# Expert results stored by SyncE in sorted order and gathered by GpSimd, in place of a scatter by GpSimd and a reload

## The reference, cut to what matters

```python
shared_enc = _expert_stack(x, sW1, sb1, sW2, sb2).sum(0)          # 128 -> 512 -> 128, gelu
weights = jax.nn.softmax(x @ gW + gb, axis=-1)                    # 15 experts
topv, topi = jax.lax.top_k(weights, TOP_K)                        # TOP_K = 3
gated = (jax.nn.one_hot(topi, E_ROUTER) * topv[..., None]).sum(axis=-2)
router_out = _expert_stack(x, rW1, rb1, rW2, rb2)                 # 128 -> 256 -> 128 each
router_enc = jnp.einsum('ebtd,bte->btd', router_out, gated)
return shared_enc + router_enc + x                                # then the last layer norm
```

## Time and profile before

| what | us |
|---|---|
| median of 3 timed runs | 285.67 (283.55 to 286.89) |
| the profiled execution, its span (what lies around it is not shown) | 319.6 |
| busy: PE / DVE / ACT / POOL | 241.1 / 221.6 / 192.2 / 179.0 |

### The profile page before, as it was taken

One profiled execution on the slowest core, in us unless ns is written; L12 is line 12 of the kernel. 1 busy time (PEld: TensorE's weight loads), 2 busy tenths in 40 slices (PEclk: granted clock), 3 DMA queues, 4 the chain that ended last, 5 costly groups with the idle time before them and its releaser, 6 DMA issues.

```text
span 319.6 us, 7117 instructions
## 1 busy us (share of the span) xinstructions
PE 241.1 (75%) x2283; PEld 179.8 (56%) x2283; DVE 221.6 (69%) x630; ACT 192.2 (60%) x423; POOL 179.0 (56%) x166
## 2 busy tenths in 40 slices
PE   6989989877988767996761299688868867785970
PEld 3676868655535434452451156586857757674960
DVE  6777999989999998998520497043444434856875
ACT  4697997549976976754470350344554546563665
POOL 6132755330666738985677467135656566665752
PEclk9999999999997998998978589799999999999778
DMA  7672830124000002952211133123132263354462
GB/s 218 217 213 46 181 128 2 37 67 133 2 0 2 0 4 62 378 215 49 86 58 50 44 101 108 41 61 101 53 99 76 75 187 90 91 168 123 150 185 90
DMA packets 38597, 31.89 MB, mean 100 GB/s; under 512 B 12864, under 2 KB 31552, under 8 KB 38432
## 3 DMA queue, kind: packets, MB, share of 16 engines
q1 hardware_dynamic: 34608, 23.90, 26.6%
q0 software_dynamic: 3520, 7.27, 6.7%
q10 hardware_dynamic: 432, 0.27, 0.3%
HBM read 19.95 MB, written 11.47 MB: 98 GB/s over the span
## 4 chain that ended last, share of the span: by engine, by line
PE 44%; DVE 27%; issue 14%; ACT 4%; another core or an unknown queue 4%; POOL 4%; DMA 1%; DVEq 0%; SPq 0%; ACTq 0%
PE psum L994 12%; PE psum L985 9%; PE psum L783 5%; DVE prob_sums L1496 4%; PE psum L763 4%; DVE maxes L1490 3%; PE psum L977 2%; PE psum L568 2%; DVE prob_sums L1410 2%; POOL x_srt L1986 2%; PE psum L585 1%; DMA xT<-x_t 1%; DVE turned_room L1421 1%; DVE maxes L1405 1%
## 5 line engine op out<-in xcount | busy, mean ns | idle before, releaser
L2047 POOL DMA_INDIRECT y_tok<-k_heads,y_rows x62 | 62.7, 1012 | 50.8 <-ACT k_heads L1327 34.4
L1319 ACT ACTIVATE k_heads<-psum,k_heads 128x128 f32<-128x128 f32 x124 | 38.7, 365 | 38.5 <-PE psum L985 33.6
L1986 POOL DMA_INDIRECT x_srt<-v_blocks,slot x48 | 48.0, 1000 | 21.3 <-issue 17.2
L994 PE MATMUL psum<-k_heads 128*128 128x128 f32 x248 | 42.4, 295 | 18.0 <-issue 12.1
L1823 DVE COPY k_heads<-psum 128x128 f32<-128x128 f32 x62 | 17.8, 289 | 48.9 <-PE psum L977 32.7
L994 PEld LDWEIGHTS psum<-k_heads 128*128 128x128 f32 x248 | 34.2, 200 | 21.9 <-issue 15.2
L985 PE MATMUL psum<-k_heads 128*128 128x128 f32 x248 | 40.6, 288 | 5.2 <-DVE k_heads L1823 4.2
L1963 POOL TENSOR_TENSOR k_heads<-k_heads,inv_sums 128x1024 f32<-128x1024 f32 x14 | 27.1, 1939 | 24.0 <-DVE inv_sums L1503 23.9
L985 PEld LDWEIGHTS psum<-k_heads 128*128 128x128 f32 x248 | 33.8, 198 | 8.5 <-DVE k_heads L1823 7.4
L1951 POOL TENSOR_TENSOR probs<-probs,inv_sums 128x512 f32<-128x512 f32 x16 | 16.8, 1050 | 28.9 <-DVE inv_sums L1415 28.7
L1327 ACT ACTIVATE k_heads<-psum,k_heads 128x128 f32<-128x128 f32 x62 | 22.9, 370 | 11.3 <-PE psum L994 9.1
(11 more groups left out here) (191 smaller groups left out, 530.1 us busy)
## 6 DMA issues: line engine op xcount, KB each, us to landing
expert_w<-e_w SPq DMA_DIRECT2D x1, 4369.0 KB
k_heads<-x_srt SPq DMA_DIRECT2D x62, 65.0 KB
q_heads<-y_tok SPq DMA_DIRECT2D x8, 256.0 KB
x_srt<-pad SPq DMA_DIRECT2D x16, 65.0 KB
xT<-x_t SPq DMA_DIRECT2D x4, 256.0 KB, 5.1
ctxT_k<-ctx_k SPq DMA_DIRECT2D x2, 512.0 KB, 5.5
v_scr<-v_rows SPq DMA_DIRECT2D x4, 256.0 KB, 2.8
ctxT_v<-ctx_v SPq DMA_DIRECT2D x2, 512.0 KB, 5.0
```

Source lines behind the costliest of these rows:

```text
L994: mm = pe.matmul(bank[6 + t % 2][:, 0:E], h_tile[:, t % 2, a, :], tile_weights(t)[:, FE + E * a:FE + E * a + E], start=(a == 0), stop=(a = ...
L1319: ins = act.activation(h_tile[:, t % 2, a, :], bank[2 + t % 2][:, P * a:P * a + P], ACT.Gelu, bias=tile_weights(t)[:, EW - 2 + a:EW - 1 + a])
L1986: pool.indirect_dma_start(out=x_srt, out_offset=bass.IndirectOffsetOnAxis(ap=slot[:, n:n + 1], axis=0), in_=payloads[:, g, k, :], in_offse ...
L2047: pool.indirect_dma_start(out=y_tok, out_offset=bass.IndirectOffsetOnAxis(ap=y_rows[:, t:t + 1].bitcast(mybir.dt.uint32), axis=0), in_=y_t ...
```

## The change

- A result is no longer scattered. SyncE stores each tile's 128 result rows as they are to `y_srt` in DRAM, in the order of the tiles (one plain DMA per tile, four semaphores in turn). SyncE therefore issues two DMAs per tile: the load of tile t + 8 and the store of tile t.
- When all tiles of a quarter are stored (counts in `t_landed`, now for all four quarters), GpSimd gathers the quarter's results with 12 indirect DMAs of 128 rows, by the same slots that the rows were scattered with. The reload is gone.
- The gate is applied when the results are summed: twelve operations of 128 columns per quarter in place of three of 512. The last quarter is summed, with its statistics, row block by row block. The third quarter's sum and all scaling by the layer norm come after the loop.
- The payloads are gone: rows of 128 elements are scattered straight from `x2`, and the scatter waits for slots and `x2` only.
- SyncE stores the padding row early, ahead of the x1 stores; it makes four register loads for late rows in place of eight, and the first twelve to sixteen tiles can be loaded before the last scatters.
- The first-stage matmuls of the shared expert's last quarter (with their gelus) move from ahead of the loop to tiles 20, 21, 23 and 24, its second stage to tiles 28, 31, 34 and 37.
- The final stores of three quarters are issued by SyncE after its last result store.

```diff
-        SUMS_AT = (39, 48, 57)
-        ROOTS_AT = 52
-        SHARED_TILES = (8, 14, 20, 26)
+        SUMS_AT = (42, 57)
+        SHARED_IN_TILES = (20, 21, 23, 24)
+        SHARED_TILES = (28, 31, 34, 37)
...
+            sp.wait_ge(s_router_ready, 1)
+            sp.dma_start(x_srt[NE * ROOM:NE * ROOM + P, :], pad[:, :]).then_inc(s_filled, 16)
...
-            sp.wait_ge(s_router_ready, 5)
-            sp.dma_start(x_srt[NE * ROOM:ROWS, :], pad[:, :]).then_inc(s_filled, 16)
...
-            rows_of = [sp.value_load(t_late[0:1, k:k + 1], ...) for k in range(NB)]
+            rows_of = [sp.value_load(t_late[0:1, k:k + 1], ...) for k in range(LATE)]
...
+            def x_loaded(t, rows):
+                if t < 4 * LATE:
+                    if t % 4 == 0:
+                        sp.wait_ge(s_late_rows, rows_of[t // 4])
+                elif t == 4 * LATE:
+                    sp.wait_ge(s_late_rows, late_rows)
+                sp.dma_start(x_tile[:, t % NB, :], x_srt[bass.ds(rows[t % 4], P), :]).then_inc(s_x_tile[t % NB], 16)
+
+            def y_stored(t, rows):
+                sp.wait_ge(s_y_tile, t + 1)
+                if t >= NY:
+                    sp.wait_ge(s_y_stored[t % NY], 16 * (t // NY))
+                sp.dma_start(y_srt[bass.ds(rows[t % 4], P), :], y_tile[:, t % NB, :].bitcast(I32)).then_inc(s_y_stored[t % NY], 16)
+
+            for t in range(NB):
+                if t % 4 == 0:
+                    x_rows_at = x_row_of(t)
+                x_loaded(t, x_rows_at)
             for t in range(NT):
+                if t + NB < NT:
+                    if t % 4 == 0:
+                        x_rows_at = x_row_of(t + NB)
+                    sp.wait_ge(s_tile_turned, t + 1)
+                    x_loaded(t + NB, x_rows_at)
                 if t % 4 == 0:
-                    row_of = nc.values_load_multi_w_load_instructions(
+                    y_rows_at = row_of(t)
+                y_stored(t, y_rows_at)
+            for c in range(NC - 1):
+                for g in range(4):
+                    sp.wait_ge(s_final, 4 * c + g + 1)
+                    store(sp, c, g)
...
+            def shared_in_late(n):
+                k, a = 6 + n // 2, n % 2
+                if n == 0:
+                    pe.wait_ge(s_acc, NC - 1)
+                    pe.wait_ge(s_ends, 2)
+                if n >= 2:
+                    pe.wait_ge(s_h_shared, 4 * (NC - 1) + n - 1)
+                pe.matmul(bank[4 + a], expert_w[:, NE + k % 2, P * a:P * a + P], x2T[:, 512 * (NC - 1):512 * NC],
+                          start=True, stop=True).then_inc(s_shared_psum, 1)
...
-            pe.wait_ge(s_h_shared, 4 * NC)
+            pe.wait_ge(s_h_shared, 4 * (NC - 1))
...
-                        act.wait_ge(s_y_scattered[t % NB], 16 * (t // NB))
-                    act.activation(y_tile[:, t % NB, :], bank[6 + t % 2][:, 0:E], ACT.Copy,
-                                   scale=x_tile[:, t % NB, E:E + 1]).then_inc(s_y_tile, 1)
+                        act.wait_ge(s_y_stored[t % NY], 16 * ((t - NB) // NY + 1))
+                    act.copy(y_tile[:, t % NB, :], bank[6 + t % 2][:, 0:E]).then_inc(s_y_tile, 1)
...
+                for g in range(4 * c, 4 * c + 4):
+                    ins = dve.scalar_tensor_tensor(out=acc[:, g, :], in0=routed_y[k][:, g, :], scalar=gate_cols[:, g, k:k + 1],
+                                                   in1=acc[:, g, :], op0=ALU.mult, op1=ALU.add)
...
+            def added_last(j):
+                g = 4 * (NC - 1) + j
+                dve.wait_ge(s_y_last[j], 16 * TOPK)
+                for k in range(TOPK):
+                    routed(dve.scalar_tensor_tensor(out=acc[:, g, :], ...))
+                routed(dve.bn_stats(bn3[:, g, :], acc[:, g, :]))
+                dve.bn_aggr(mean_var3[:, g, :], bn3[:, g, :]).then_inc(s_y_sum, 1)
...
                     if n % 12 == 0:
                         pool.wait_ge(s_slots, g // 4 + 1)
-                        pool.wait_ge(s_payload_gates, g // 4 + 1)
-                        pool.wait_ge(s_payloads, 2 * (g // 4) + 2)
+                        pool.wait_ge(s_x2, g + 4)
...
-            for t in range(NT):
-                pool.wait_ge(s_y_tile, t + 1)
-                pool.wait_ge(s_y_rows, t // 4 + 1)
-                pool.indirect_dma_start(out=y_tok, ...)
+            for c in range(NC):
+                for k in range(NY):
+                    pool.wait_ge(s_y_stored[k], landed[c][k])
+                pool.sem_inc(s_y_through, 1)
+                for n in range(4 * TOPK * c, 4 * TOPK * (c + 1)):
+                    g, k = n // TOPK, n % TOPK
+                    pool.indirect_dma_start(out=routed_y[k][:, g, :].bitcast(I32), out_offset=None, in_=y_srt,
+                                            in_offset=bass.IndirectOffsetOnAxis(ap=slot[:, n:n + 1], axis=0)
+                                            ).then_inc(s_y_got[c] if c < NC - 1 else s_y_last[g % 4], 16)
```

More of the change, by code:

```diff
@@ L70 @@
 RUNS = NL * NE
-DONE_BY = tuple((4 * P * TOPK * (c + 1) + NE * (P - 1)) // P for c in range(NC))
 SOON = (NC - 1) * 4 * TOPK
 NB = 8
+NY = 4
 NS = 5
-XW = E + 2
-ROWS = NE * ROOM + P
+LATE = 4
+ROWS = NE * ROOM + TABLE * P
 K_IOTA, K_BASE, K_T, K_TP, K_J = 0, NE, 2 * NE, 2 * NE + TABLE, 2 * NE + 2 * TABLE
@@ L462, in _ @@
             sp.wait_ge(s_scattered, 16 * (SOON - 1))
-            for t in range(NT):
-                if t % 4 == 0:
-                    row_of = nc.values_load_multi_w_load_instructions(
[L466 to L489, removed]
@@ L490, in _, with row_of @@
-            for g in range(4):
-                sp.wait_ge(s_final_v, g + 1)
[L492 to L503, removed]
+            def row_of(t):
+                return nc.values_load_multi_w_load_instructions(
+                    tile_of(t, 0), engines=[SP], min_val=0, max_val=ROWS - P,
+                    skip_runtime_bounds_check_because="the table ends at the last tile's row")[1]
@@ new lines, in x_row_of @@
+            def x_row_of(t):
+                return nc.values_load_multi_w_load_instructions(
+                    tile_of(t, 2), engines=[SP], min_val=0, max_val=NE * ROOM,
+                    skip_runtime_bounds_check_because="the table ends at the last tile's row")[1]
+            def x_loaded(t, rows):
[5 more added lines that the diff above has]
+                sp.dma_start(x_tile[:, t % NB, :], x_srt[bass.ds(rows[t % 4], P), :]).then_inc(s_x_tile[t % NB], 16)
@@ L504, in _ @@
+            for c in range(NC - 1):
+                for g in range(4):
+                    sp.wait_ge(s_final, 4 * c + g + 1)
+                    store(sp, c, g)
+            for g in range(2):
+                sp.wait_ge(s_final_v, g + 1)
                 store(sp, NC - 1, g)
@@ L1827, in tiles_landed @@
             def tiles_landed():
-                routed(dve.tensor_copy(done_count[:, :], more_sum[0:1, NL - 1:NL + 1, NE - 1]))
-                for n in range(2):
-                    routed(dve.tensor_scalar(used_f[:, :], row_consts[0:1, K_T:K_T + TABLE], done_count[:, n:n + 1], 16.0,
-                                             ALU.is_lt, ALU.mult))
-                    with nc.allow_low_precision(reason="whole numbers below 2**24"):
-                        ins = dve.tensor_reduce(t_landed[0:1, n, :], used_f[:, :].rearrange("p (j k) -> p k j", k=NB), AX_X, ALU.add)
-                    if n == 0:
-                        routed(ins)
@@ L1837, in tiles_landed @@
-                ins.then_inc(s_landed, 1)
+                routed(dve.tensor_tensor(used_f[:, :, :], row_consts[0:1, K_T:K_T + TABLE].unsqueeze(1).broadcast_to([1, NC, TABLE]),
+                                         more_sum[0:1, NL + 1 - NC:NL + 1, NE - 1:NE].broadcast_to([1, NC, TABLE]), ALU.is_lt))
+                routed(dve.tensor_scalar(used_f[:, :, :], used_f[:, :, :], 16.0, None, ALU.mult))
+                with nc.allow_low_precision(reason="whole numbers below 2**24"):
+                    dve.tensor_reduce(t_landed[0:1, :, :], used_f[:, :, :].rearrange("p c (j k) -> p c k j", k=NY),
+                                      AX_X, ALU.add).then_inc(s_landed, 1)
@@ L1851, in sum_stats, with last_stats @@
+            def last_stats():
+                gs = slice(4 * (NC - 1), NG)
+                dve.wait_ge(s_y_sum, 4 * (NC - 1) + 4)
+                dve.tensor_scalar(var_eps3[:, gs], mean_var3[:, gs, 1], EPS, None, ALU.add).then_inc(s_ln3, 1)
+                dve.wait_ge(s_ln3, 2 * (NC - 1) + 1)
+                dve.reciprocal(rstd3[:, gs], var_eps3[:, gs]).then_inc(s_ln3, 1)
             def sum_stats(c):
@@ L1920, in _ @@
                     expert_of = expert_staged(t + 2, expert_of)
+            root_seed(0, NC - 2)
+            for n in range(3):
+                root_newton(0, NC - 2)
+            sum_mean(0, NC - 2)
+            for k in range(TOPK):
+                added(NC - 2, k)
+            sum_stats(NC - 2)
             root_seed(NC - 2, NC - 1)
@@ L1926, in _ @@
             sum_mean(NC - 2, NC - 1)
```

(8 more changed lines are left out.)

149 lines of the change are left out of this document (51 added, 98 removed).

## The result

The changed kernel takes 296.02 us (median of 4 runs, 293.31 to 297.41), the kernel before 285.85 beside it: the ratio is 1.038, 95% interval 1.033 to 1.044, so it is slower by 10 us where the forecast had 4.5.

A forecast was written before the change was run, and what follows sets the result against it. GpSimd was taken as the bound from 158 us on. The end moves from R + 81.8 to R + 87.2, 5.4 later, less 0.9 at the first row scatter: 285.67 + 5.4 - 0.9 = 290.2 us, range 279 to 300.

The forecast's parts named there:

- R: End of the 48 row scatters on GpSimd, from which schedules are counted; forecast undisturbed at 196.2 us.
- second wait: GpSimd's wait for tile 45 after 24 gathers; forecast had tile 45 stored at R + 47.3, just in time.
- SyncE's pace: Tile loop: two DMAs of 0.54 and a wait of 0.06 make 1.15 us a tile, so SyncE paces.
- the third: Rival, SyncE saturates in the tile loop: 1.40 us a tile, tile 45 stored at R + 58.3, 300.8 us; chance 0.10.
- the schedule of before: Undisturbed schedule of the kernel before: GpSimd scatters 1.26 us apart, 54 in 68.0, then 13.8; end R + 81.8.
- rival 2: GpSimd after R + 17.4: gathers cheaper than scatters, 283.4 us at 1.00 apart, 276.4 at 0.54; chance 0.25.
- the end behind the last gather: After the 48 gathers: landing, three last sums, statistics, hand-offs and the old 5.2 us, together 9.25 us.
- VectorE and stores: Quarter sums of twelve 0.28 us operations cost 1.3 more, off the bound; twelve final stores through near R + 76.
- the 0.9 us at the front: GpSimd's first row scatter no longer waits for gates: idle time 1.16 becomes 0.30 us, a gain of 0.9.
- The cover for the shared matmuls: Tile loop: SyncE 0.15 us a tile slower than TensorE, 3 us over 20 tiles; without it tile 45 up to 3.6 late.
- the sum at the traced pace: Schedule at 1.65 us a tile, loop starting 3.6 earlier without shared matmuls: 322.9 against 319.6 us, 3.3 later.
- The sign named for wrong: One of the signs that would show the forecast wrong: a profile of the changed kernel shorter than 316 us.

The follow-up runs named there:

- one table load: Changed kernel with one of two register loads per four tiles left out on SyncE for the 48 never-padding tiles: 292.25 us (1.035).
- both reliefs: Changed kernel with one register load of two left out and every third result store issued by ScalarE's queue instead of SyncE's: 292.69 us (1.025).
- and shared matmuls late: Changed kernel with a register load left out, every third store on ScalarE's queue, and the last quarter's shared matmuls behind tile 45: 287.97 us (1.007).
- the run with five waits: Changed kernel with five more, long satisfied waits on SyncE behind every result store: 305.24 us (1.075).

## Why the prediction was right in direction and short in size

Times from R; "19th" and "45th" are the issue of these stores:

| | first store | 19th | first gather | 45th | second wait | end |
|---|---|---|---|---|---|---|
| forecast | -5.6 | 15.1 | 17.4 | 45.0 | none | 87.2 |
| changed kernel | -5.1 | 21.9 | 24.4 | 57.6 | 4.9 | 98.8 |
| one table load | -5.3 | 19.8 | 22.4 | 53.1 | 3.2 | 95.7 |
| both reliefs | -5.6 | 17.3 | 19.8 | 52.1 | 4.5 | 94.4 |
| and shared matmuls late | -5.4 | 16.0 | 19.3 | 44.5 | none | 89.9 |

- *The step that failed: "SyncE's pace", 1.15 a tile.* The mechanism was the one on record (two DMAs a tile on one queue, GpSimd idle until 19 tiles are stored); the term was mis-sized. It measured 1.50 for the first 19 tiles and 1.43 to tile 45. 0.12 of it is counting: I took 0.54 per transfer from eight loads "with the table load in it", but there one table load stands beside eight transfers and in the loop two do, which is 0.33 / 4 = 0.08 a tile; the other 0.04 is what transfers and waits cost above 2 x 0.54 + 0.06. That 0.06 for a wait had no row behind it; the run with five waits shows 0.06 for each of the three instructions that hold them. The other 0.16 to 0.23 are mainly long issues, and a late row scatter, which those eight loads did not contain. Over 44 tiles 1.15 against 1.43 is 12.2 us; the last gather ends 12.5 later than forecast and the end is 11.6 later.
- *A price from the Trainium skill.* The Trainium skill (DMA: Bandwidth & Descriptors, Latency and other measured facts) puts a register load at a floor of about 600 ns; by that the prediction had an estimate of 1.30 a tile and 296 us, close to what came. The trace disagrees with the floor: the 32 table loads have a median of 0.30 us. The nearness is luck. An overpriced load stood in for stalls that I had left out, and 1.30 counts the loads too low: with two loads of 0.60 in four tiles and the eight loads' 4.34 less their one table load, the estimate by the page is some 1.37 a tile and 299.
- *The rival that happened* is the third, SyncE at 1.40. Its after-schedule, R + 97.8, is within 1 us of the measured one. By its mechanism it is right in part: both table loads and the waits make 1.27, and the long issues, which it did not have, most of the rest. Its 300.8 was too late because the schedule of before was too short: R + 81.8 against 86.2, of which 2.6 is VectorE being busy ahead of the last sums and 1.9 the scatters' pace. The forecast's difference between the two schedules, 5.4, thus misses 11.6 - 4.4 = 7.2: the error in the schedule of before hides a part of the other.
- *Right:* a gather costs what a scatter does (1.25 to 1.26 apart), which ends rival 2; the first store at R - 5.6 (R - 5.1); the end behind the last gather, 9.25 (8.4).
- *VectorE and stores:* a sum's operation takes 0.35 us where I had 0.28, the last three of them some 0.2 more; the twelve stores that follow SyncE's last result are issued by 282.6, before the last sums, as said.
- *Not to be resolved:* the 0.9 us at the front. The first row scatter's idle time did go from 1.16 to 0.18, but R lies between 193.1 and 198.0 in the traces of the changed kernel and its variants, more than the gain.
- *The cover for the shared matmuls* was named right (SyncE slower than TensorE). What its loss costs was too small: up to 3.6 us in the prediction, for the first stage alone, and 6.3 measured with both stages moved. The 3.6 us that the sum at the traced pace gave the loop's start had no counterpart: with these matmuls back in front the first gather is where it was.
- *The sign named for wrong,* a profile under 316 us, came true (293.8) and means little: the profile of before was held up, and the changed kernel's trace has 1.43 us a tile where that schedule had 1.65.

## What to carry to other kernels

When work moves to a queue that "only issues", count each instruction in its steady state, register loads and waits too, at the rate at which the loop holds them, and multiply by the tiles up to the first consumer: here 0.28 us a tile were 12 us. An engine that must wait for the slowest of many producers before its first transfer pays for the whole ramp; fewer operations on it pay only if they outweigh that. And an engine that is full in the windows need not be the bound: ask the queue behind it whether it waits for results. The same matmuls were worth at most 0.9 us and then 6.3.

## What was not expected of the hardware

Most of SyncE's long issues fall together with single packets of a queue that the profile calls "instruction". For the issue of 1.58 us at 206.01, the transfers from 205.8 to 207.7 (the first row is the DMA engines' busy share in 40 slices, in tenths):

```profile
DMA  9035245676434578652100000000000010001000
...
q8 instruction: 1, 0.02, 4.6%
```

and for the one of 1.92 us at 192.61, from 192.5 to 194.6:

```profile
DMA  8892000994233599630000000000000019992113
...
q8 instruction: 1, 0.02, 4.5%
```

In both the data transfers all but stop, for 0.6 and 0.7 us, and one packet of 0.02 MB falls in the stretch. The stop may be no more than a result of the issue's: what SyncE does not issue is not moved. The window without a long issue, from 207 to 220, has no packet that begins in it. The packets come at intervals of 11 to 19 us in the loop; beside the one at 224.70 no issue is long. What they hold, and whether they or something with them lengthen the issue, was not tried; the long issues are a part of the 1.43 that no run here removed.

Also new here: instructions added to lengthen an engine's work must be looked for in the trace. Register loads that nothing reads were gone from it (32 table loads with and without them), and five waits in a row stand in it as three instructions.
